# Attention with 16 heads of 16 features: value products of eight heads per step, row maxima turned as a full tile, and new orders of steps

## The reference, cut to what matters

```
x = x + attn_A(layernorm(x))          # causal, weights and inputs quantised to 8 bits
x = x + attn_X(layernorm(x), ctx)     # 120 context keys, a mask, and one more key that is all zero
x = x + block_F(layernorm(x))         # layernorm, attention, layernorm, then routing to the experts
attention:  scores = q k^T / 4;  p = softmax(scores);  out = (p v) W + b
```

## Time and profile before

| what | us |
|---|---|
| median of 3 executions (5688.51 to 5694.07) | 5688.54 |
| the profiled execution, its own time | 5689.64 |
| its span, first to last instruction | 5687.9 |
| busy in the span: PE | 5301.0 (93%) |
| PEld | 4213.5 (74%) |
| DVE | 4520.0 (79%) |
| ACT | 3673.0 (65%) |
| POOL | 2070.8 (36%) |

### The profile page before, as it was taken

How to read it: one execution, slowest core, us unless ns; L and a number is a source line. 1 busy time by engine, 2 the same in 40 slices (tenths; PEclk the granted TensorE clock), 3 DMA queues, 4 the chain that set the end, 5 groups by cost and what they waited for, 6 DMA issues and landing times. The chain is left out here.

```text
span 5687.9 us, 155750 instructions
## 1 busy us (share of the span) xinstructions
PE 5301.0 (93%) x47387; PEld 4213.5 (74%) x47388; DVE 4520.0 (79%) x12198; ACT 3673.0 (65%) x8251; POOL 2070.8 (36%) x1753
## 2 busy tenths in 40 slices
PE   0899999979999999799999999995899999999998
PEld 0677777757777777567777777761799999899997
DVE  7889998867777777588888888878777777677776
ACT  4788888858888888577777776764344444444443
POOL 0322222223344333244444444430344444344443
PEclk9999999989999999999999999995899999999999
DMA  5677777746666666466666666652222322222321
GB/s 157 173 183 184 183 184 183 183 124 185 184 186 184 184 183 186 122 168 180 178 168 180 178 169 178 179 144 6 65 57 42 57 50 44 53 47 43 58 41 26
DMA packets 631736, 751.04 MB, mean 132 GB/s; under 512 B 143363, under 2 KB 560332, under 8 KB 631472
## 3 DMA queue, kind: packets, MB, share of 16 engines
q1 hardware_dynamic: 575136, 679.62, 45.9%
q0 software_dynamic: 49152, 63.10, 6.9%
q10 hardware_dynamic: 7184, 5.00, 0.4%
HBM read 476.49 MB, written 272.24 MB: 132 GB/s over the span
## 5 line engine op out<-in xcount | busy, mean ns | idle before, releaser
L1853 POOL DMA_INDIRECT out_dram<-exp_gated,exp_token x256 | 425.6, 1662 | 890.1 <-DMA out_dram<-exp_gated,exp_token 325.5
L831 ACT ACTIVATE F_probs<-F_scoreT 128x512 f32<-128x512 f32 x1024 | 585.8, 592 | 233.7 <-PE F_scoreT L658 233.3
L940 DVE TENSOR_REDUCE F_tops<-F_score 128x2 f32<-128x512 f32 x1024 | 684.0, 686 | 53.4 <-PE F_score L686 36.3
L940 DVE TENSOR_REDUCE A_tops<-A_score 128x3 f32<-128x384 f32 x1024 | 528.0, 553 | 64.3 <-PE A_score L676 56.3
L831 ACT ACTIVATE A_probs<-A_scoreT 128x384 f32<-128x384 f32 x1024 | 451.1, 488 | 28.7 <-PE A_scoreT L646 15.2
L658 PE MATMUL F_scoreT<-QS,KS 98*128 98x256 bf16 x2048 | 365.5, 275 | 9.7 <-ACT F_probs L831 1.5
L686 PE MATMUL F_score<-KS,QS 96*128 96x256 bf16 x2048 | 362.9, 274 | 8.8 <-DMA KS<-d_k 7.9
L1834 POOL DMA_INDIRECT exp_x<-d_h,exp_token x256 | 281.1, 1098 | 179.3 <-DMA exp_w<-in_L_ffn_w_dram 101.7
L1630 ACT ACTIVATE exp_hT<-exp_hT,exp_b 128x512 f32<-128x512 f32 x512 | 338.6, 711 | 3.1 <-DVE exp_hT L1785 3.1
L940 DVE TENSOR_REDUCE X_tops<-X_score 128x4 f32<-128x484 f32 x512 | 323.4, 653 | 15.7 <-PE X_score L681 14.5
L831 ACT ACTIVATE X_probs<-X_scoreT 121x512 f32<-121x512 f32 x512 | 297.2, 588 | 31.4 <-PE X_scoreT L654 28.6
(11 more groups left out here) (392 smaller groups left out, 16046.8 us busy)
## 6 DMA issues: line engine op xcount, KB each, us to landing
QS<-d_q SPq DMA_DIRECT2D x384, 192.0 KB, 3.7
KS<-d_k SPq DMA_DIRECT2D x256, 192.0 KB, 4.0
QS<-d_q SPq DMA_DIRECT2D x384, 128.0 KB, 3.9
KS<-d_k SPq DMA_DIRECT2D x256, 128.0 KB, 4.0
d_q<-A_q_parts SPq DMA_DIRECT2D x64, 384.0 KB, 3.5
d_k<-A_k_parts SPq DMA_DIRECT2D x64, 384.0 KB, 3.9
QS<-d_q SPq DMA_DIRECT2D x384, 64.0 KB, 3.6
d_q<-X_q_parts SPq DMA_DIRECT2D x64, 384.0 KB, 2.7
```

The source lines that it names most:

```text
L831: nc.scalar.activation(probs[m % 2][0:KR, at:at + HB, :].rearrange("p u x -> p (u x)"), scoreT[i % TB][0:KR, 0:HB * TCOL], ACT.Exp)\
L940: nc.vector.tensor_reduce(dst, src, AX.X, ALU.max).then_inc(score_read, 1)
L1853: nc.gpsimd.indirect_dma_start(out, bass.IndirectOffsetOnAxis(token[j % (2 * XB)][:, s:s + 1], 0), gated[par][:, s, :], None, bounds_check ...
```

## The change

Value products: a step now takes eight heads, so there are two steps (`pv0`, `pv1`) and two copies (`evac0`, `evac1`) per batch instead of four. `outs` becomes [128, 512], the whole bank; within a step, heads 4a + j share column tile j and take columns 256a to 256a + 255. Each `probs` buffer holds eight heads. The number of matmuls is the same. Row maxima: `top_parts` become the first 32 columns of a tile of 128 that is set to zero once at the start of each stage, and the whole tile is turned. Orders: all five lists of all three kinds are written anew, and in A `k_store` and `q_rest` move from lag 3 to lag 2. In the diff below only the orders of PE, ACT, DVE and SP that the text speaks of are shown.

```diff
     "A": {
-        "SP": ("rowsB fetch loadA rowsA tok1 loadB q_store k_store"),
-        "PE": ("v attend pv3 maxima attend maxima maxima rowsB attend attend tok0 maxima maxima attend xT attend "
-              "maxima tok1 q pv0 attend maxima k maxima attend attend maxima maxima attend pv1 maxima rowsA "
-              "maxima attend attend maxima attend attend pv2 attend maxima attend maxima maxima"),
+        "SP": ("rowsB k_store fetch tok1 loadA rowsA loadB q_store"),
+        "PE": ("v pv1 attend maxima attend maxima rowsB maxima attend attend maxima xT attend maxima tok0 attend "
+              "maxima q attend tok1 maxima attend maxima maxima k attend pv0 maxima rowsA attend maxima attend "
+              "attend maxima maxima attend attend maxima attend attend maxima maxima"),
...
     "X": {
-        "PE": ("v pv3 attend maxima rowsB maxima tok0 attend tok1 maxima xT0 attend ctxT aT maxima xT1 attend yT "
-              "q maxima maxima wo attend pv0 k attend proj rowsA pv1 maxima attend pv2 maxima attend"),
-        "ACT": ("seed seed evac3 q_rest rowsB attend seed k_rest attend xT0 seed ctxT aT xT1 seed yT seed attend "
-              "q attend seed attend attend evac0 k rowsA evac1 seed attend evac2 attend"),
+        "PE": ("v pv1 maxima attend rowsB maxima tok0 attend tok1 maxima xT0 attend ctxT aT maxima xT1 attend yT "
+              "q maxima wo attend k maxima attend proj rowsA pv0 maxima attend attend maxima"),
+        "ACT": ("seed seed seed evac1 q_rest k_rest rowsB attend seed attend xT0 ctxT aT xT1 attend seed yT seed "
+              "q attend attend attend seed k rowsA seed evac0 attend attend"),
...
     "F": {
-        "PE": ("attend v pv3 attend attend maxima maxima attend attend maxima rowsB attend tok0 maxima tok1 "
-              "attend maxima xT attend maxima pv0 aT maxima maxima q maxima proj attend maxima rowsA attend pv1 "
-              "attend h2T maxima attend attend maxima maxima k route maxima attend maxima attend pv2 maxima "
-              "attend"),
+        "PE": ("v attend attend maxima pv1 attend maxima maxima attend rowsB attend maxima tok0 attend tok1 "
+              "maxima attend xT attend maxima aT maxima maxima q maxima proj maxima attend maxima rowsA attend "
+              "pv0 attend h2T maxima attend maxima attend maxima k attend maxima route maxima attend attend"),
...
-SHIFTED = {"A": {},
+SHIFTED = {"A": {"k_store": 2, "q_rest": 2},
...
-        outs = ps("outs", [P, 256])
-        probs = [sb(f"probs{i}", [P, 4, TCOL]) for i in range(2)]
+        outs = ps("outs", [P, 512])
+        probs = [sb(f"probs{i}", [P, H // 2, TCOL]) for i in range(2)]
...
-        top_parts = [sb(f"top_parts{i}", [P, 2, H // 2, 2], BF16) for i in range(2)]
+        top_wide = [sb(f"top_parts{i}", [P, P], BF16) for i in range(2)]
+        top_parts = [t[:, 0:2 * H].rearrange("p (a h j) -> p a h j", a=2, j=2) for t in top_wide]
...
-                            pe.wait_ge(probs_full, G * g + (m + 1) * 4 // HB)
-                            need(pe, outs_read, 4 * g + m)
-                            pr = probs[m % 2]
+                            pe.wait_ge(probs_full, G * g + (m + 1) * G // 2)
+                            need(pe, outs_read, 2 * g + m)
+                            pr = probs[m]
+
+                            def sums(j, a):
+                                return outs[32 * j:32 * j + 32, 256 * a:256 * a + 256]
...
                             elif kind == "X":
-                                for j in range(4):
-                                    last = mm(outs[32 * j:32 * j + 32, :], V[gp][0:KN, 0, 4 * m + j, :], pr[0:KN, j, :],
-                                              start=True, stop=True)
+                                for a in range(2):
+                                    for j in range(4):
+                                        last = mm(sums(j, a), V[gp][0:KN, 0, 8 * m + 4 * a + j, :], pr[0:KN, 4 * a + j, :],
+                                                  start=a == 0, stop=True, skip_group_check=True)
...
-                            last = nc.tensor.transpose(Wb[0:2 * H, 0:P], top_parts["AB".index(name[4])][:, :, :, :]
-                                                       .rearrange("p a h j -> p (a h j)"), ident_b[:, :])
+                            last = nc.tensor.transpose(Wb[:, 0:P], top_wide["AB".index(name[4])][:, :], ident_b[:, :])
...
                             if at == 0:
-                                need(act, pv_done, 4 * g + m - 1)
+                                need(act, pv_done, 2 * g + m - 1)
...
-                            nc.scalar.activation(outT[:, m, :], outs[:, :], ACT.Copy).then_inc(outs_read, 1)
+                            nc.scalar.activation(outT[:, 2 * m:2 * m + 2, :].rearrange("p a q -> p (a q)"), outs[:, :], ACT.Copy).then_inc(outs_read, 1)
...
             def _(dve):
+                for t in top_wide:
+                    nc.vector.memset(t[:, :], 0.0).then_inc(padded, 1)
+                dve.wait_ge(padded, 2)
```

More of the change, by code:

```diff
@@ L310 @@
+        "ACT": ("q_rest evac1 attend attend attend rowsB attend xT attend attend attend q attend k attend rowsA "
+              "attend evac0 attend attend attend attend k_rest attend attend"),
+        "DVE": ("topB maxima v maxima maxima maxima maxima tok0 maxima tok1 maxima maxima topA maxima maxima "
               "maxima norm maxima maxima maxima maxima maxima"),
-        "POOL": ("q k q_rest k_rest"),
+        "POOL": ("q_rest q k k_rest"),
     },
     "X": {
-        "SP": ("fetch loadB mload rowsB q_store refetch k_store ctxT stats loadA rowsA proj"),
@@ L315 @@
-        "PE": ("v pv3 attend maxima rowsB maxima tok0 attend tok1 maxima xT0 attend ctxT aT maxima xT1 attend yT "
-              "q maxima maxima wo attend pv0 k attend proj rowsA pv1 maxima attend pv2 maxima attend"),
-        "ACT": ("seed seed evac3 q_rest rowsB attend seed k_rest attend xT0 seed ctxT aT xT1 seed yT seed attend "
-              "q attend seed attend attend evac0 k rowsA evac1 seed attend evac2 attend"),
-        "DVE": ("mcopy topB v maxima tok0 tok1 norm maxima maxima maxima topA wo stats maxima aggr maxima var c0 "
-              "c1 c2 proj c3 c4 c5 maxima c6 c7 c8 maxima c9 c10 apply"),
+        "SP": ("fetch loadB mload rowsB q_store k_store refetch ctxT loadA stats rowsA proj"),
@@ L394, in attention @@
     LAG = {"loadA": 2, "loadB": 2, "mload": 2, "mcopy": 1, "v": 1, "maxima": 1, "seed": 1, "topA": 1, "topB": 0, "rowsA": 1, "rowsB": 0,
-           "attend": 0, "pv0": 0, "pv1": 0, "pv2": 0, "evac0": 0, "evac1": 0, "evac2": 0,
-           "pv3": -1, "evac3": -1, "refetch": -1, "tok0": -1, "tok1": -1, "aT": -1, "proj": -1,
+           "attend": 0, "pv0": 0, "evac0": 0, "pv1": -1, "evac1": -1, "refetch": -1, "tok0": -1, "tok1": -1, "aT": -1, "proj": -1,
            "ustats": -1, "uaggr": -1, "uvar": -1, "uapply": -1, "h2T": -2, "route": -2,
@@ L491, in attention @@
                               "scoreT_full", "probs_full", "pv_done", "outs_read", "link_v", "result_out"))
+        padded = sem("padded")
         stack_in = [sem(f"stack_in{h}") for h in range(2)]
@@ L698, in _ @@
                             if kind == "A":
-                                for n in range(2):
+                                for a in range(2):
                                     for j in range(4):
-                                        o = outs[32 * j:32 * j + 32, :] if n == 0 else outs[32 * j:32 * j + 32, P:256]
-                                        x = pr[:, j, P:384] if n == 0 else pr[:, j, 0:P]
-                                        last = mm(o, V[gp][:, n, 4 * m + j, :], x, start=n == 0, stop=n == 1,
-                                                  skip_group_check=True)
+                                        mm(sums(j, a), V[gp][:, 0, 8 * m + 4 * a + j, :], pr[:, 4 * a + j, P:384], start=a == 0,
+                                           stop=False, skip_group_check=True)
@@ L709, in _ @@
                             else:
                                 for n in range(2):
-                                    for j in range(4):
-                                        last = mm(outs[32 * j:32 * j + 32, :], V[gp][:, n, 4 * m + j, :],
-                                                  pr[:, j, n * 256:(n + 1) * 256], start=n == 0, stop=n == 1,
-                                                  skip_group_check=True)
+                                    for a in range(2):
+                                        for j in range(4):
+                                            last = mm(sums(j, a), V[gp][:, n, 8 * m + 4 * a + j, :],
+                                                      pr[:, 4 * a + j, n * 256:(n + 1) * 256], start=n + a == 0, stop=n == 1,
+                                                      skip_group_check=True)
@@ L1038, in _ @@
                             dve.wait_ge(work_full[bank], use + 1)
-                            need(dve, pv_done, 4 * (g - 1))
```

(1 more changed line is left out.)

32 lines of the change are left out of this document (18 added, 14 removed).

## The result

The kernel after takes 5643.62 us (median of four, 5639.62 to 5645.5), the kernel before 5691.31 on the same chip: a ratio of 0.9915 [0.9901, 0.993], a gain of 48 us. The forecast was 5549 with a range of 5500 to 5615. The direction was right; a third of the gain came.

A forecast was written before the change was run, and what follows sets the result against it. PE's list of steps was taken to bound A and F, and PE's list plus PE-ACT waits X; 64 x (0.76 + 0.62 + 0.80) = 139.5 us less 1 for memsets gave 5549 us, range 5500 to 5615.

The forecast's parts named there:

- A value-product step pays about 0.22 us: On PE, each value-product step costs 0.22 us beside its matmuls; two fewer per batch save 0.44 us.
- 0.19 us per rows step: On PE, tile changes around each narrow turn lose 0.19 us; two full-array turns save 0.38 us a batch in A and F.
- How much of PE's gain reaches the time: Share of PE's saving reaching each batch: 0.76 of 0.82 us in A, 0.62 in X, 0.80 of 0.82 in F.
- the covers of `pv0`: PE steps between the eighth head and `pv0`, said to hide its wait: two `attend` in F, one in A, two in X.
- An exponential takes 0.5 to 0.6 us: ACT's time per exponential, set against the PE steps between the last head and a value product.
- Waits for SP and POOL remain: In X, such waits limit savings of 0.66 us on PE and 0.33 on ACT to 0.62 a batch, bounds 0.33 and 0.9.
- The wider load, the copies, the memsets: Turn's wider weight load costs nothing; two 512-column ACT copies take 1.19 us against 1.52; memsets cost 1 us in all.
- Rival 2: Half sticks, as DVE or late loads hold A and ACT holds X: 77 us gained, 5612 us; chance 0.15.
- Rival 3: Slower: PE waits for a late eighth exponential at each of 384 product steps, 0.59 us each: 5776 us; chance 0.04.
- Rival 1: New orders also remove old waits, 0.4 us a batch more in all three stages: 5472 us, 5500 likelier; chance 0.17.
- Rival 4: Leaving fp32 work, not changing tile, costs the 0.2 us, so turns gain nothing: 63 us missing, 5612 us; chance 0.03.
- rival 5: PE stands for the whole 98 ns weight load at each of 384 turns: 38 us missing, 5587 us; chance 0.03.

The follow-up runs named there:

- e2: The kernel after in the old orders, the five lists of the kernel before without the dropped steps: 5803.68 us, 1.0199 of before.
- e3: The kernel after with the turns narrow again, reading only the first 32 columns: 5682.19 us, 0.9984 of before.
- e11: The kernel after without the clamp, one 0.43 us DVE operation of A's norm: 5609.34 us, 0.986 of before.
- e1: The kernel before with only the wide `top_parts` turns and their memsets: 5660.84 us, 0.9946 of before.
- e8: The kernel after with four-head steps and old orders in A, X's SP stores and POOL's fetch earlier: 5586.21 us, 0.9821 of before.
- e9: The kernel after with four-head steps and before's orders in A and X, but X's SP stores behind `mload`: 5576.89 us, 0.98 of before.
- e10: The kernel after with four-head steps and old orders in A, X's SP stores ahead of `rowsB`, behind `mload`: 5549.89 us, 0.9749 of before.
- e4: The kernel after with an `attend` fed before A's `pv1` and `evac1`, and X's SP stores right behind `loadB`: 5679.81 us, 0.9982 of before.
- e7: The kernel after with A's norm later, eighth exponential before q, `pv0` before k, X's SP stores and POOL's fetch earlier: 5744.87 us, 1.0099 of before.
- e5: The kernel after with A's DVE norm two maxima later, X's SP stores behind `loadB` and POOL's fetch before `mload`: 5676.78 us, 0.9977 of before.
- e6: The kernel after with A's eighth exponential before q, `pv0` before k, and X's POOL fetch before `mload`: 5698.81 us, 1.0018 of before.

## Why the prediction was wrong, point by point

Expected were 138.5 us, and 48 came. By stage, against 64 times the term: A was to give 0.76 us a batch and lost 0.34, 70 us; X was to give 0.62 and gave 0.20, 27 us; F gave 0.97 for 0.80, which is 11 us the other way; filling and emptying the stages cost 8.3 where 1 was taken (with the new orders: e2, which has the memsets and the old orders, has 155.2, 73.4 and 67.2 us for the 155.5, 74.4 and 67.0 of before). That is 70 + 27 - 11 + 7 = 93, against 91 missing by the medians and 94 by the profiled executions. (The prediction's own sum, 5551 less 1.1, gives 5550 and not 5549.)

**"A value-product step pays about 0.22 us" and "0.19 us per rows step": right.** The steps are 1.44, 1.87 and (in X) 1.00 us as forecast, the turn 0.06. F, whose PE has no gap in either kernel, gave more than its term. Of its 0.97 e3 gives 0.21 to the turns, not 0.38: the turn between two `attend` still costs 0.20 from start to start, no less than a narrow one there (0.16 in e3), so what stands behind it is another wait and not the tile. The rest came with products and orders, which weren't run apart in F by a version that keeps four-head steps in new orders; that they must go together e2 shows.

**"How much of PE's gain reaches the time" in A: the step that failed.** I took DVE's waits for PE as the only limit: with them gone DVE would need 15.2 us, 0.69 less, so 0.76 taken. Two things were wrong in it. First, one engine's list without its waits is a lower bound of a period and not its value when the engines are joined by short buffers: three `score` banks, two `scoreT` banks. DVE was busy for 14.2 us of a batch after (14.3 before), 88% and not the 95% forecast, and yet 0.43 us off its list was 0.44 off the period (e11), as 0.38 us of turns on PE's was 0.40 (e3). The period of A is a ring that goes through both lists. Second, the products were priced as PE's work alone. What they cost beyond that e2 shows against e1: +1.05 us a batch in A and +1.21 in F with less work on PE. The reading that fits its waits: a step of 1.44 us is also 1.44 us in which PE makes no scores; with two `scoreT` and three `score` banks, each used up in about half a microsecond, ACT and DVE stand still and then PE waits for them (for ACT's exponentials 121 us in A's 50 batches in e2, 31 in 54 in e1). The same steps in the new orders leave A 0.60 us above four-head steps (after against e8). I had named the covers of `pv0` one by one and never asked what a product of double length starves.

**"An exponential takes 0.5 to 0.6 us", one `attend` between the eighth head and `pv0` in A: counted on the wrong engine.** I counted PE's steps between score and use. On ACT the eighth exponential stands behind 1.67 us of q's copies, so PE waits 0.42 us at each `pv0` (18.9 us in 52 cases; 1.6 us in 2 before). "Its own cover" has to be counted in the list of the engine that does the work.

**"Waits for SP and POOL remain" in X: named and not priced.** I took 0.62 with bounds of 0.33 and 0.9, and 0.20 lay below the lower one. X was bound by the order of SP's queue in both kernels: e1 shortened PE's list and moved nothing, a changed order of SP's list alone gave 0.54 with the steps of the kernel before (e9 against e1), and two stores moved gave 0.76 with those of the kernel after (e10). The 0.20 that did come can't be put down to PE's 0.66: SP's list changed as well. The queue's view was read for A alone; SP's list has its own period, and the share of its DMAs (0.67) doesn't show it. Of the lower bound: it was worked out from ACT's saved copies and thus again from an engine whose time was not the limit.

**The wider load, the copies, the memsets: right.** The load took 96 ns (92 before), the copies 0.594 us, the turn takes 0.06 from start to start, and e2, with the memsets, writes V first at 155.2 us (155.5 before). That leaves no room for an unhidden load, and the 31 us that the prediction worked out from the Trainium skill (TensorE: Matmul & The Clock Gate, LDWEIGHTS) did not appear: that page would have the load grow from 27 to 107 ns.

**The rivals.** Rival 2, half of it sticks, was nearest in kind (DVE in A, little in X) but priced at 5612, since it left A a gain. Rival 3's mechanism is real at one of A's two products a batch: 0.42 us each, above its point of decision of 0.36 a step if it had come at all 384; it came at 64 of them in A, 27 us at most. Rival 1, more gain, fell. Rival 4 (no price of a tile) fell by e1, rival 5 (the load) by the row. What the range lacked was a case in which one stage gets slower while the others gain: rival 3 was priced for all three stages at once, and so looked improbable.

**Open.** Why no order tried makes eight-head steps pay in A is shown only in part. Six were run (after, e2, e4 to e7); three of them (e5, e6, e7) ran into POOL, so they don't tell what the norm's place or the wait at `pv0` is worth. An order that avoids both, e2 with ACT's exponential ahead of the copy, or a third `scoreT` bank in place of one of the three `score` banks, wasn't tried.

## What to carry to other kernels

Fewer and longer steps save a fixed price each, but a step's length is also the time in which the engine feeds nobody: compare it with what the buffers between the engines hold. Where two engines are near 90% and joined by two or three buffers, test for a ring before summing: take a known piece off each list (e3, e11) and see whether the period follows one for one. And list the period of every in-order queue, the one that issues DMAs too, before a gain is put down to an engine.

## What the runs showed of the hardware

Some operations of DVE from SBUF to SBUF (`TENSOR_SCALAR`, `TENSOR_TENSOR`, `CAST`) stood when an operation of POOL had started before them, and ended with it or shortly behind: 0.48 to 1.55 us for 512 columns beside `xb` (e5), 0.17 to 1.05 for eight columns (e6), with ends 0.29 and 0.02 us after POOL's, and a `CAST` of 16 columns in X, after, up to 1.25 where it takes 0.18 alone. The order of the starts mattered: in e5 the first of A's rescaling operations of 512 columns (L971) began before POOL's in all 46 cases and kept its 486 ns, the next (L973) began behind it and took 1280. The reductions from PSUM didn't stretch: after, in A, 183 of them lay wholly beside an operation of POOL, with a median of 550 ns, and 841 did not, with 552. Nor did `BATCH_NORM_STATS2` in X, which reads SBUF (428 ns with POOL's operation first). Both kernels have such waits in A: one of the two subtractions of eight columns takes 0.37 us before (0.16 alone) and 0.66 after, and one operation of the norm 0.65 before (0.40 alone and after), so they come to about the same and don't explain what A lost. But I hadn't expected them, and they came with a worse order twice, in e5 and e6. SBUF — State Buffer (Who interferes with whom) of the Trainium skill says that DVE in a mode of two ports and GpSimd share a pair of ports, that whoever issues first has it for the whole instruction and the other is blocked, that `tensor_scalar` and casts can enter such a mode, and that a DVE instruction with two inputs in SBUF contends with a GpSimd instruction that reads SBUF. The trace agrees, with the numbers above; it doesn't show in which mode an operation ran.
